# Feed-forward weights loaded directly behind the tokens, and quantised before the tokens' pieces

## Time and profile before

| what | value |
|---|---|
| median of 3 runs | 622.52 us (621.84 to 622.91) |
| the profiled execution's own time | 622.93 us |
| its span, first to last instruction | 621.2 us |
| busy: PE, DVE, POOL, ACT | 90%, 89%, 87%, 65% |
| mean granted clock of TensorE | 0.987 |

### The profile page before, as it was taken

One profiled execution on the slowest core, in us unless ns is written; L12 is line 12 of the kernel. 1 busy time (PEld: TensorE's weight loads), 2 busy tenths in 40 slices (PEclk: granted clock), 3 DMA queues, 4 the chain that ended last, 5 costly groups with the idle time before them and its releaser, 6 DMA issues.

```text
span 621.2 us, 11230 instructions
## 1 busy us (share of the span) xinstructions
PE 558.1 (90%) x3746; PEld 252.1 (41%) x3797; DVE 551.6 (89%) x1165; ACT 400.7 (65%) x868; POOL 540.7 (87%) x409
## 2 busy tenths in 40 slices
PE   5999498999898989998989898988989898998885
PEld 4677364444343424333423333342334343332323
DVE  5999498999999999899999989998999999997662
ACT  4677337676766666656667575667656667668793
POOL 7378669989999999898999999999988898897983
PEclk9999889999999999999999999999999999999997
DMA  5334442201000001100000000000000000000000
GB/s 154 103 98 110 137 76 70 60 35 46 2 3 1 1 2 50 45 1 2 2 2 0 19 1 1 2 2 1 2 2 1 19 0 2 1 1 2 1 2 18
DMA packets 14833, 16.68 MB, mean 27 GB/s; under 512 B 1639, under 2 KB 14216, under 8 KB 14360
## 3 DMA queue, kind: packets, MB, share of 16 engines
q1 hardware_dynamic: 14240, 15.70, 9.1%
q10 hardware_dynamic: 536, 0.26, 0.2%
HBM read 11.75 MB, written 4.01 MB: 25 GB/s over the span
## 4 chain that ended last, share of the span: by engine, by line
PE 47%; POOL 22%; DVE 11%; ACT 9%; issue 5%; SPq 4%; DMA 1%; ACTq 1%; POOLq 0%; another core or an unknown queue 0%; DVEq 0%
POOL ring L894 16%; PE psum L1465 13%; PE psum L1423 10%; PE psum L1447 8%; DVE mxp L1238 6%; ACT ring L1048 2%; PE psum L1398 2%; PE psum L1379 2%; POOL xw L912 2%; POOL xw L910 2%; DVE ring L1265 2%; PE psum L1381 2%; PE psum L1450 1%; POOL xw L914 1%; SPq L666 1%
## 5 line engine op out<-in xcount | busy, mean ns | idle before, releaser
L894 POOL TENSOR_TENSOR ring<-ring,dist 128x1024 f32<-128x1024 f32 (+3 forms) x223 | 436.9, 1988 | 36.5 <-ACT ring L1048 36.2
L1238 DVE TENSOR_REDUCE mxp<-psum 128x1 f32<-128x512 f32 (+3 forms) x640 | 355.3, 601 | 21.2 <-PE psum L1423 16.8
L1048 ACT ACTIVATE ring<-psum 128x512 f32<-128x512 f32 (+3 forms) x446 | 212.0, 529 | 121.9 <-PE psum L1450 68.1
L1423 PE MATMUL psum<-kop,qop 96*128 96x512 bf16 (+3 forms) x640 | 199.7, 352 | 5.7 <-DVE mxp L1238 2.5
L1447 PE MATMUL psum<-qop,kop 128*128 128x512 bf16 (+3 forms) x590 | 178.0, 346 | 18.0 <-DVE mxp L1238 11.4
L1465 PE MATMUL psum<-ring,vaug 128*32 128x512 f32 (+3 forms) x1280 | 150.0, 539 | 15.1 <-POOL ring L894 13.3
L1265 DVE TENSOR_TENSOR ring<-psum,dist 128x512 f32<-128x512 f32 (+3 forms) x194 | 116.7, 627 | 12.7 <-ACT psum L1048 12.5
L1048 ACT ACTIVATE psum<-psum 128x512 f32<-128x512 f32 (+3 forms) x194 | 101.0, 552 | 35.3 <-PE psum L1450 15.9
L1423 PEld LDWEIGHTS psum<-kop,qop 96*128 96x128 bf16 x640 | 57.9, 98 | 123.2 <-DVE mxp L1238 41.0
L1447 PEld LDWEIGHTS psum<-qop,kop 128*128 128x128 bf16 x640 | 59.5, 97 | 91.1 <-DVE mxp L1238 24.4
L1426 PE MATMUL psum<-tri_q,identb 128*128 128x128 bf16 x256 | 55.9, 221 | 0.0
(11 more groups left out here) (134 smaller groups left out, 468.4 us busy)
## 6 DMA issues: line engine op xcount, KB each, us to landing
parts_dram<-qpart SPq DMA_DIRECT2D x18, 128.0 KB, 3.2
kop<-parts_dram SPq DMA_DIRECT2D x6, 384.0 KB
qop<-parts_dram SPq DMA_DIRECT2D x6, 384.0 KB
xin<-_attn_hidden_states_dram SPq DMA_DIRECT2D x4, 256.0 KB, 4.9
ring<-inv_dram SPq DMA_DIRECT2D x1, 1024.0 KB, 4.9
out_dram<-xin SPq DMA_DIRECT2D x4, 256.0 KB, 2.3
qop<-parts_dram SPq DMA_DIRECT2D x3, 288.0 KB
kop<-parts_dram SPq DMA_DIRECT2D x3, 288.0 KB
```

Source lines behind the costliest of these rows:

```text
L894: g_.tensor_tensor(slot(p)[:, :, 0:n], slot(p)[:, :, 0:n], both, ALU.mult).then_inc(weighed_pool, 1)
L1048: a_.activation(scores if pair_vec[p] else slot(p)[:, e % 2, 0:n], scores, ACT.Exp, scale=SCALE).then_inc(exp_done, 1)
L1238: v_.tensor_reduce(mxp[:, u % 2, 4 * a + j, c - g:c - g + 1], bank(*o)[:, 0:n], AX_X, ALU.max).then_inc(max_used, 1)
L1423: ins = mm(bank(*o)[:, 0:n], qop[0:K_MAX, u // NQ % 2, h, P * a:P * (a + 1)], kop[0:K_MAX, h, k0:k0 + n], start=True, stop=(c != g))
```

## The change

It loads the weights right behind the tokens and the small list, ahead of the wait for that list and of `hankel`. The weights become pieces 0 to 2 and the tokens pieces 3 to 6. The plan now takes the weights as landed at 9500 ns. `WARM` falls from 20 to 14. POOL no longer clears all 768 columns of the gate and up part of `xw` before the loads, but only the 32 partitions by 256 columns that no load writes; so the loads need not wait for it, and DVE's first stage of a weight piece waits for it instead.

```diff
-W_PIECES = [4, 5, 6]
-X_PIECES = [0, 1, 2, 3]
+W_PIECES = [0, 1, 2]
+X_PIECES = [3, 4, 5, 6]
...
-WARM = 20
+WARM = 14
...
-WEIGHTS_AT = 62000
+WEIGHTS_AT = 9500
...
             sp.dma_start(inv_dram.rearrange("(p n) -> p n", p=P), invd[:]).then_inc(inv_stored, 16)
+            for m, w in enumerate((w_gate, w_up)):
+                o = S + 3 * P * m
+                sp.dma_start(xw[:, o:o + 2 * P].rearrange("p (t k) -> p t k", t=2),
+                             w[0:2 * P, :].rearrange("(t p) k -> p t k", p=P)).then_inc(w_loaded, 16)
+                sp.dma_start(xw[0:F - 2 * P, o + 2 * P:o + 3 * P], w[2 * P:F, :]).then_inc(w_loaded, 16)
+            sp.dma_start(xw[:, S + 6 * P:XW], w_down).then_inc(w_loaded, 16)
+            sp.dma_start(wp[:], w_proj).then_inc(w_loaded, 16)
+            sp.dma_start(bv[:], b_attn[2 * D:3 * D].rearrange("(p o) -> p o", o=1)).then_inc(late_loaded, 16)
+            sp.dma_start(wdT[F - 2 * P:F - 2 * P + 1, 2], b_proj.rearrange("(a n) -> a n", a=1)).then_inc(late_loaded, 16)
             sp.wait_ge(inv_stored, 16)
             sp.dma_start(hankel, bass.AP(inv_dram.tensor, 0, [[1, P], [1, S]])).then_inc(hankel_loaded, 16)
...
-                    if c == GROUPS[1]:
-                        sp.wait_ge(zeroed, 1)
-                        for m, w in enumerate((w_gate, w_up)):
...
-            g_.memset(xw[:, S:S + 6 * P], 0.0).then_inc(zeroed, 1)
+            pool.wait_ge(vones_ready, 2)
+            third = xw[F - 2 * P:P, S:S + 6 * P].rearrange("p (m t k) -> p m t k", m=2, t=3)[:, :, 2]
+            g_.memset(third, 0.0).then_inc(zeroed, 1)
+            pool.wait_ge(zeroed, 1)
...
                         vec.wait_ge(w_loaded, 16 * N_W)
+                        vec.wait_ge(zeroed, 1)
```

## The result

The changed kernel takes 604.13 us (median of 4 runs, 602.84 to 605.48) against 622.57 us before: ratio 0.9706, 95% interval 0.9676 to 0.9736. The profiled execution took 605.48 us, with a span of 603.8 us.

The account below looks back on a forecast made before the run. DVE, with POOL close by, sets the pace of a long steady stretch. Profiled 622.93 - 7.97 (stall) + 0.5 (POOL's backlog) - 0.5 (bank) - 1.3 (start) = 613.7 us; median forecast 613.4, range 609.5 to 618.

Parts of the forecast that it names:

- The stall and its cause: DVE's wait at 67.72 us for the weight loads, queued behind keys and queries at SP; its removal gains 7.97 us.
- POOL's backlog: Work POOL did under the stall must find room elsewhere: 0.5 us given back, bounds 0 and 2.7.
- The start: With 14 warming transposes PE takes the normalised tokens at 8.70 us: 1.3 us gained, bounds 1.3 gained to 0.4 lost.
- rival A: Projections of q and k run at PE's lower clock, 0.9 to 1.7 us given back: 614.3 to 615.1, chance 0.13.
- The work is the same ... Bounds 0 and about 2 us of gain; I take 0.5: Pieces change places: the first attention unit's normalisation goes earlier and frees a PSUM bank sooner, 0.5 us gained.
- Rival B: New order misfits in the steady part: 618.5 us (0.08), 623 to 627 (0.05), or good side 609 to 611 (0.08).
- Rivals C and D: C: stall only moves, to the second group's key loads, 617.5 us, chance 0.04; D: no change, 622 to 623, 0.02.

Follow-up runs that it names:

- ten orders: Early loads, WARM 20, weights last or first, planner's input unaltered or one of four constants 1 ns higher: means 611.3 us (last) and 606.9 (first).
- experiment 1: The changed kernel with pieces back in the order of before and WARM at 20, so only the loads move early: 613.59 us, ratio 0.9852 against before.

## Why the prediction was wrong

- *The stall and its cause*: right. L1137's wait and the place in SP's queue made the hole, and the early loads cost nothing at the start (`hankel` 0.26 us later, no wait for it). Its size was too small: the early loads alone gave 8.4 us by the medians and a lead of 9.5 us in the profiles, instead of 7.97 less 0.5 for POOL's backlog. The prediction gave the stall the length of DVE's wait and left out that PE's clock had fallen during it, although the granted clock of 0.60 stood in the earlier trace rows and PE had fillers to run ahead of the first `pv`.
- *The start*: the forecast took 1.3 us of gain; rival A came true in the changed kernel (projections at 1062 ns). The Trainium skill ("TensorE: Matmul & The Clock Gate", Part 1) says that the warm-up is a span of time and no number of matmuls, and that it varies from run to run. The traces agree: with the same PE list up to there the passes took 1062 ns in the changed kernel, 1061 in its repeat, and 592 in the kernel before with 14. The part was worth nothing (the changed kernel took 604.13 us with 14 and 604.20 with 20).
- *"The work is the same ... Bounds 0 and about 2 us of gain; I take 0.5"*: this is the step that failed. It priced the new place of the pieces by what lies next to them, and not by the orders, which are all written anew behind the 76th of PE's items. It was worth 9.4 us (613.59 to 604.20 in the same rounds): about 4.4 with the order of the pieces and 5.0 by luck, as far as ten orders tell. How the order of the pieces makes its part is open.
- *Rival B* named the mechanism and said that it "can equally come out on the good side: 609 to 611", with a chance of 0.08. The mechanism was right, and the term was mis-sized. The ten orders show a spread of 5.6 to 6.4 us within one kind, so a range for a kernel with such a planner should be some 3 us wider on each side, and nothing in these runs makes the good side less likely than the bad one.
- *Rivals C and D*: behind 40 us no wait of PE's ends on a load (the longest of all is 1.1 us, for POOL), and the change was not hidden.

## What to carry to other kernels

When every engine stands still ahead of a stretch that is full to the end, the stall's removal can be worth its length in full, as here, and the slow clock behind it too; look at the granted clock of the windows that follow. Where a planner writes the orders, any edit to its input draws a new order: perturb the input by next to nothing a few times on both sides, and compare means, before a gain is credited to an idea. A lead won ahead of a stall that ends on a transfer's arrival is lost in it (1.06 us became 0.34), so small edits at the start are to be measured after the stall is gone.

## What the runs showed that was not expected

- Six transposes fewer (3.25 us of warming in place of 4.53) left the projections at the lower clock in both profiles of the changed kernel (1062 ns a pass), and not in the profile of the kernel before with the same edit (592 ns), though PE's list is the same up to there.
- In before PE idled from 69.44 to 76.90; its granted clock was at the lower level from about 72.0 to 82.1, and the same PE work took 2.3 us longer in that stretch than in experiment 1.
- The planner's sensitivity: 1 ns in one of its constants moved the kernel by 5.6 us (604.20 to 609.80).
